# Perceiver block on one core: the broadcast shift read from PSUM, the transposed maxima in a score bank

## The reference, cut to what matters

```
qp = q @ Wq.T + bq;  kp = ctx @ Wk.T + bk;  vp = ctx @ Wv.T + bv
scores = (qp @ kp.T) * scale              # 512 x 8192, scale = 32 ** -0.5
attn = softmax(scores, axis=-1)
x = x + (attn @ vp) @ Wo.T + bo
```

## Time and profile before

| | |
|---|---|
| median of 3 runs | 548.07 us (547.96 to 549.03) |
| the profiled execution | 548.39 us |
| its span, first to last instruction | 546.3 us |
| PE busy | 538.7 us, 99% |
| DVE busy | 345.9 us, 63% |
| ACT busy | 256.8 us, 47% |
| POOL busy | 197.4 us, 36% |
| granted PE clock | 1.00 throughout |

### The profile page before, as it was taken

The page is one execution under the profiler, slowest core; times in us unless marked ns, Lnnn a source line. Parts: engine busy times, 40 slices in busy tenths (PEclk is TensorE's granted clock), DMA queues, the critical chain, the costliest instruction groups (busy, mean ns, idle before and its releaser), DMA issues.

```text
span 546.3 us, 7076 instructions
## 1 busy us (share of the span) xinstructions
PE 538.7 (99%) x2612; PEld 451.8 (83%) x2612; DVE 345.9 (63%) x574; ACT 256.8 (47%) x421; POOL 197.4 (36%) x125
## 2 busy tenths in 40 slices
PE   8999999999999999999999999999999999999997
PEld 7998887788888888888888888888878888888886
DVE  5745555866477655557986546998536226638757
ACT  5624346745445545454455435575355452562210
POOL 3860421312211143232212433385099709800000
PEclk9999999999999999999999999999999999999999
DMA  8602432342232224222223123423302203300002
GB/s 326 245 28 77 158 112 74 126 148 78 86 145 78 77 79 146 86 77 78 91 91 127 40 77 128 180 81 123 145 0 62 93 1 119 113 1 1 0 2 77
DMA packets 14002, 51.61 MB, mean 94 GB/s; under 512 B 1680, under 2 KB 1680, under 8 KB 13072
## 3 DMA queue, kind: packets, MB, share of 16 engines
q1 hardware_dynamic: 13968, 51.16, 26.3%
HBM read 50.11 MB, written 1.05 MB: 94 GB/s over the span
## 4 chain that ended last, share of the span: by engine, by line
PE 95%; ACT 2%; DVE 2%; issue 1%; DMA 1%; DVEq 0%
PE bank L1195 28%; PE bank L1267 11%; PE bank L1269 11%; PE bank L1268 11%; PE bank L1256 10%; PE bank L1258 10%; PE bank L1257 10%; PE bank L1185 1%; PE bank L1423 1%; DMA xs<-x 1%; PE bank L1432 0%; ACT xn L548 0%; DVE xT_l L806 0%; PE bank L1295 0%; PE bank L1551 0%
## 5 line engine op out<-in xcount | busy, mean ns | idle before, releaser
L457 POOL TENSOR_TENSOR cn_l<-raw_n,cn_h 128x1024 fp32r<-128x1024 f32 x32 | 80.1, 2502 | 207.9 <-ACT cn_h L587 207.9
L886 DVE TENSOR_TENSOR top<-top,bank 128x512 f32<-128x512 f32 x60 | 41.2, 687 | 101.1 <-ACT ring L611 100.8
L1256 PE MATMUL bank<-qk_h,ct_h 128*128 128x512 f32 x256 | 100.1, 391 | 1.1 <-DVE top L886 1.1
L1267 PE MATMUL bank<-ph,cn_h 128*128 128x512 f32 x256 | 100.4, 392 | 0.0
L1269 PE MATMUL bank<-ph,cn_l 128*128 128x512 f32 x256 | 99.7, 390 | 0.0
L1258 PE MATMUL bank<-qk_h,ct_l 128*128 128x512 f32 x256 | 99.7, 389 | 0.0
L1268 PE MATMUL bank<-pl,cn_h 128*128 128x512 f32 x256 | 99.7, 389 | 0.0
L1257 PE MATMUL bank<-qk_l,ct_h 128*128 128x512 f32 x256 | 99.7, 389 | 0.0
L611 ACT COPY ring<-bank 128x512 f32<-128x512 f32 x64 | 37.5, 586 | 75.1 <-PE bank L1258 75.1
L621 ACT ACTIVATE ph<-ring 128x512 fp32r<-128x512 f32 x64 | 40.4, 632 | 65.1 <-PE bank L1269 47.4
L913 DVE TENSOR_TENSOR ring<-ring,shift_b 128x512 f32<-128x512 f32 x64 | 60.4, 949 | 2.0 <-ACT shift_b L632 2.0
(11 more groups left out here) (213 smaller groups left out, 900.2 us busy)
## 6 DMA issues: line engine op xcount, KB each, us to landing
raw_t<-ctx_t SPq DMA_DIRECT2D x32, 512.0 KB, 4.2
raw_n<-ctx_n SPq DMA_DIRECT2D x32, 512.0 KB, 3.3
piece_raw<-pieces SPq DMA_DIRECT2D x12, 512.0 KB, 3.3
xs<-x SPq DMA_DIRECT2D x4, 256.0 KB, 3.8
wq_raw<-wq_t SPq DMA_DIRECT2D x4, 256.0 KB, 4.5
wk_raw<-wk_in SPq DMA_DIRECT2D x1, 1024.0 KB, 7.0
wvo_raw<-wv_t SPq DMA_DIRECT2D x1, 1024.0 KB, 12.0
wvo_raw<-wo_t SPq DMA_DIRECT2D x1, 1024.0 KB, 7.1
```

Of the source, the lines that this page charges most:

```text
L457: pool.tensor_tensor(cn[p % CNB][1][:], raw_n[p % 2][:], cn[p % CNB][0][:].bitcast(F32), ALU.subtract).then_inc(cnl_ready, 1)
L1256: pe.matmul(bank[:, dst, :], ct[i // 2 % 2][0][:, c, keys], qk[0][:, c, :], start=(c == 0), stop=False)
L1267: pe.matmul(bank[:, c, :], keys[0][:, q % 2, d], ph[q % PB][:], start=first, stop=False)
```

## The change

It has five parts.

1. `transpose_top` writes the transposed maxima to bank 5 (the new TOP_BANK, the second score bank), and `new_shift` reads them there. At that point the last tile of bank 5 has been read, and the next one, `scores(s + 1)`, isn't written yet. So `scores(i)` with i = 17, 33 and 49 has a new wait for top_step, which is at its value when DVE has finished the reduction. `exponents` into bank 5 has a wait of the same kind.
2. `lower_by_shift` reads the shift from bank 7 itself, where it was broadcast, and not from the SBUF copy `shift_b`. The copy is still made (for `shrink`), and the subtraction still waits for it (shiftb_ready).
3. Because bank 7 is now read until the block's last subtraction, `transpose_shift(n)` waits for sub_done, the count of subtractions, to reach 16 n; `transpose_top` no longer waits for shiftb_ready (bank 7 isn't its target any more).
4. `lowered_by` has the subtractions one tile further ahead (four tiles instead of three), but not across a block's end.
5. On DVE, `new_shift` moves ahead of `low_p`, `add_den` and `low_ct` of its step.

```
@@ constants
+        TOP_BANK = S_BANKS[1]
@@ exponents(q), on ACT
                 if p_bank(q) == S_BANKS[1]:
                     act.wait_ge(max_done, TILES)
+                    act.wait_ge(top_step, 4 * (NSB - 1) + 1)
@@ new_shift(n), on DVE
-                dve.reduce_max(block_max[:], bank[:, MISC, :].rearrange("p (t k) -> p t k", t=TT),
+                dve.reduce_max(block_max[:], bank[:, TOP_BANK, :].rearrange("p (t k) -> p t k", t=TT),
@@ lower_by_shift(q), on DVE
-                dve.tensor_tensor(ring[:, q % RING, :], ring[:, q % RING, :], shift_b[q // SB % 2][:],
+                dve.tensor_tensor(ring[:, q % RING, :], ring[:, q % RING, :], bank[:, MISC, :],
                                   ALU.subtract).then_inc(sub_done, 1)
@@ lowered_by(k), on DVE
                 if n != NSB - 2 or k + LEAD < 0:
-                    return min(k + LEAD + 1, TILES)
+                    return min(k + LEAD + 2, (n + 1) * SB, TILES) if k + LEAD >= 0 else 0
@@ the loop of DVE
+                if s % SB == 0 and s > 0 and s // SB <= NSB:
+                    new_shift(s // SB - 1)
                 if 0 <= k + LEAD - 1 < TILES:
                     low_p(k + LEAD - 1)
                     add_den(k + LEAD - 1)
                 if s % 2 == 0 and 2 <= s // 2 + 1 < NP:
                     low_ct(s // 2 + 1)
-                if s % SB == 0 and s > 0 and s // SB <= NSB:
-                    new_shift(s // SB - 1)
@@ scores(i), on PE
+                if i % SB == 1 and i > SB:
+                    pe.wait_ge(top_step, 4 * (i // SB - 1) + 1)
@@ transpose_top(n), on PE
                 pe.wait_ge(max_done, (n + 1) * SB)
-                if n == 0:
-                    pe.wait_ge(init_done, 1)
-                else:
-                    pe.wait_ge(shiftb_ready, n)
-                transpose_tile(top[n % 2][:].unsqueeze(1), 0, MISC).then_inc(top_psum, 1)
+                transpose_tile(top[n % 2][:].unsqueeze(1), 0, TOP_BANK).then_inc(top_psum, 1)
@@ transpose_shift(n), on PE
                 pe.wait_ge(top_step, 4 * (n + 1))
+                if n == 0:
+                    pe.wait_ge(init_done, 1)
+                wait(pe, sub_done, n * SB)
```

More of the change, by code:

```diff
@@ L1284, in transpose_top, with transpose_shift @@
                 pe.wait_ge(max_done, (n + 1) * SB)
+                transpose_tile(top[n % 2][:].unsqueeze(1), 0, TOP_BANK).then_inc(top_psum, 1)
+            def transpose_shift(n):
+                pe.wait_ge(top_step, 4 * (n + 1))
                 if n == 0:
                     pe.wait_ge(init_done, 1)
-                else:
-                    pe.wait_ge(shiftb_ready, n)
-                transpose_tile(top[n % 2][:].unsqueeze(1), 0, MISC).then_inc(top_psum, 1)
-            def transpose_shift(n):
-                pe.wait_ge(top_step, 4 * (n + 1))
+                wait(pe, sub_done, n * SB)
                 for t in range(TT):
```

## The result

The median is 549.35 us (548.73 to 549.80, 20 runs) against 548.22 us for the kernel before (547.90 to 549.03, 20 runs): ratio **1.0018**, 95% interval 1.0011 to 1.0025, or +1.1 us. The forecast was 549.2 and +1.11. A profiled execution took 549.62 us, span 547.5, against 548.39 and 546.3.

The account below looks back on a forecast made before the run. PE was taken to bound the kernel. The one nonzero term, a new 1.11 us wait at scores(17), was added to the 548.07 us median of earlier runs, giving 549.2 us, +0.20%; range 547.9 to 550.3.

Parts of the forecast that it names:

- What bounds: PE, busy 538.7 of 546.3 us; DVE or ACT time counts only where PE waits for it.
- the most that the loop can give back is 1.4 us: Loop over the context tiles: PE's late starts at 94.22 and 97.89 lose 1.39 us together, 0.25% of the time.
- The new wait, +1.11 us: First block's end: scores(17) waits for the DVE reduction and starts at 83.30 in place of 82.19.
- Cover at the second and third block: At scores(33), 12 matmuls of values(10) hide the wait with 1.74 us to spare; the third boundary is built alike.
- The losses at steps 21 and 22 don't absorb it: Both losses, 1.39 us, stay because their chain moves with PE by 1.11 us; the opposite rival had chance 0.11.
- Part 5, "covered by 0.4 us": At scores(18), low_ct and the peak now come behind new_shift, ready at 85.7 against a start at 86.1.
- Part 5 at step 32: The operations behind new_shift end near 160.4; scores(34) needs them at 163.78, so 3.4 us to spare.
- Part 2: Subtraction on DVE falls from 949 to 686 ns, 16.8 us less work; ACT's wait almost goes; cost to PE 0.
- Parts 3 and 4: Earlier subtractions let the shift's transposes go unheld; the one added at step 19 fits 2.61 us of DVE idle time: cost 0.
- The chances: Whole kernel: faster 0.05, same 0.48, slower 0.47, with the limit of about 0.2% at 549.17 us.
- POOL's work as what holds a subtraction up: Possible cause of held subtractions on DVE, such as 2.31 us against 0.68; POOL is idle until 90.55.
- The extra cycles of a PSUM source: Subtraction on DVE: 120 fixed cycles against 58 for SBUF would add 4.1 us over 64, not reaching PE.

Follow-up runs that it names:

- e6: Kernel before, with one tiny exponent on ACT at step 9 so the exponent's table loads early; 547.34 us, ratio 0.9985 to the kernel before.
- e11: Kernel before, with the early table load and, in step 20, the score tile's copy and maximum put first; 546.60 us, ratio 0.9972.
- e2: Kernel before, with only the transposed maxima moved to bank 5 and the new wait of the scores; 549.55 us, ratio 1.0025.
- e5: Changed kernel, with five more reductions, results unused, ahead of the second block's reduction; 551.46 us, ratio 1.0059 to the kernel before.
- e4: Changed kernel, with one more reduction, result unused, ahead of the first block's reduction; 550.22 us, ratio 1.0036 to the kernel before.
- e1: Changed kernel, but the first block's maxima are transposed into bank 7 as before; 548.81 us, ratio 1.0016 to the kernel before.
- e9: Changed kernel, with the first block's maxima in bank 7 and new_shift at its old place on DVE; 548.21 us, ratio 1.0003.
- e12: Kernel before, with only new_shift moved ahead of low_p, add_den and low_ct on DVE; 548.86 us, ratio 1.0018.
- e3: Changed kernel, but the subtraction reads the SBUF copy of the shift again; 549.37 us, ratio 1.0021 to the kernel before.

## Why the prediction was right

- **What bounds.** PE, with 1.39 us of loss in the whole loop by the prediction's count. e6 took out part of it and gained 0.9 us, e11 all of it and gained about 1.5. The stretch of e11 is 1.62 us shorter, so "the most that the loop can give back is 1.4 us" was a little low: the second matmul after each wait also starts late, 0.31 us after the first in place of 0.23, and the count left that out. With it the two losses come to 1.56 us. The change freed 17 us of DVE, moved some of ACT's waiting from the subtraction to add_den, and gained nothing.
- **The new wait, +1.11 us.** Measured 1.12 in the trace and 1.13 between the medians; e2, with that part alone, has 1.13 in the trace. The forecast of 549.2 is 0.15 low because the three runs it started from had a median of 548.07, and the twenty later ones 548.22. The 0.14 us from the end of the DVE operation to PE's start, read from two other waits, was 0.15 here.
- **Cover at the second and third block.** The reduction ended at 157.00 + 0.69 = 157.69 and scores(33) started at 159.56; less 0.14 that is 1.73 us to spare (1.74 forecast). e5 used it up and paid the excess.
- **The losses at steps 21 and 22 don't absorb it.** They stood unchanged at 95.44 and 99.11 (rows below), and in e4 they were unchanged under a delay of 1.7 us:

```profile
95.44 0.46 PE L1261 MATMUL bank<-qk_h,ct_h 128*128 128x512 f32 x1 [0.40 <-DVE top L888]
...
99.11 0.47 PE L1261 MATMUL bank<-qk_h,ct_h 128*128 128x512 f32 x1 [0.67 <-DVE top L888]
```

- **Part 5, "covered by 0.4 us".** True: 86.25 - 85.58 - 0.14 = 0.53. What the prediction didn't draw out is that the cover was the new wait itself; e1, e9 and e12 show that part 5 has a cost of its own of 0.7 us. I walked into that with e1, whose expectation took it as nothing.
- **Part 5 at step 32.** The peak of tile 32 ended at 161.38, scores(34) started at 165.00: 3.5 us to spare, 3.4 forecast.
- **Part 2.** 680 ns forecast as 686, DVE 328.6 us forecast as 329. That ACT's wait for the subtraction goes was right, but I put it to the shorter subtraction; e3 shows that it goes without that too, and ACT's wait for add_den grew by 9.2 us in its place. The cost of 0 for PE was right within what a time can show.
- **Parts 3 and 4.** The cost of 0 was right for the change as a whole: the first block's last subtraction ends at 161.30 + 0.68 = 161.98, in step 33, and the transposes that wait for it start at 167.72. But the prediction priced part 4 apart from part 2, by the idle time in step 19. e3 shows that the added subtraction in its SBUF form is held there, at a cost to PE of 0.12 us; it is free only with part 2.
- **The chances.** The ratio of 1.0018 lies just under the limit of 0.2%; same and slower had 0.48 and 0.47, and that was the honest state of it. The interval, 1.0011 to 1.0025, holds the limit too, so on which side of it the ratio fell was luck; that the loss is 1.1 us was not.

## What to carry to other kernels

On an engine that is busy 99% of the time, list the few places where its next start is late, and price a change by those alone. In this kernel 17 us less work beside it were worth nothing, 1.3 us of a table load in the wrong place were worth 0.9. When a result takes the bank that the very next product needs, look for what stands between the two on the bound engine: one tile of other work hid the wait at two boundaries, and at the one without it the whole latency was paid. Of two delays at neighbouring starts only the larger was paid, so undoing one of them left the other to be seen; price each alone.

## What the runs showed of the hardware

Of three things here the prediction only guessed at the first (POOL's work as what holds a subtraction up), expected the second, and did not foresee the last. When the subtraction had one operand in PSUM, it was never held (675 to 689 ns over 64), and POOL's subtractions got shorter too, from a median of 2548 to 2406 ns: in the kernel before both sides had paid. e3, which changes this operand alone, has both back (2887 ns at most, and a POOL median of 2560). The same place in the loop, the kernel before and then the changed one:

```profile
256.85 3.48 DVE L913 TENSOR_TENSOR ring<-ring,shift_b 128x512 f32<-128x512 f32 x2
257.24 2.54 POOL L457 TENSOR_TENSOR cn_l<-raw_n,cn_h 128x1024 fp32r<-128x1024 f32 x1 [9.89 <-ACT cn_h L587]
```

```profile
258.07 1.28 DVE L915 TENSOR_TENSOR ring<-ring,bank 128x512 f32<-128x512 f32 x2
258.45 2.40 POOL L457 TENSOR_TENSOR cn_l<-raw_n,cn_h 128x1024 fp32r<-128x1024 f32 x1 [6.37 <-ACT cn_h L588]
```

In the kernel before ten of the 64 subtractions were held (2233 ns or more), and each of the ten started while such a POOL operation was already running; those that started ahead of one took 0.68 us. The held one here ends at 256.85 + 3.48 = 260.33, 0.55 us after POOL's end at 257.24 + 2.54 = 259.78, so within a subtraction's own length of it. low_ct, which kept its two SBUF operands, is still held at times in the changed kernel (2431 ns at most, median 1219). The Trainium skill ("SBUF — State Buffer", section "Who interferes with whom") says that a DVE instruction with two SBUF inputs contends with a GpSimd instruction that reads SBUF, and that one with at most one SBUF input does not, outside the modes in which DVE uses two ports. The traces agree, with 2884 ns at most for the first form and 689 for the second. It costs both engines time here, though neither cost was felt in the time of the kernel.

Reading one operand from PSUM instead of SBUF had no price: median 680 against 684 ns. The extra cycles of a PSUM source that the prediction took from the Trainium skill ("VectorE: DVE Perf Modes", section on the TRN2 errata), 62 or about 65 ns by its estimate, do not appear.

Five extra reductions with a small output in DVE's program went, in both placements, with about 1.2 us more between DVE's last operation and the end of the span (3.6 and 3.7 us in place of 2.5). The cause stays open.
